# One part of k squared moved ahead of a z, the last row's order rewritten, and attention weights times v computed as 64x64 blocks

## What is computed

```
mod = silu(c) @ wmod                     # shifts, scales and gates, one set for each row
h   = layernorm(x) * (1 + ca) + sa
q, k, v = split(h @ w_qkv + b_qkv)       # 8 heads of 64 channels
scores  = einsum("bhld,bhle->bhde", q, k) / 8       # 64 x 64 for each head: channel by channel
attn    = softmax(scores)
a   = einsum("bhld,bhde->bhle", v, attn) @ w_fc + b_fc + h
x   = x + ga * (layernorm(a) * gamma + beta)
h   = layernorm(x) * (1 + cb) + sb
xr, xk = mixes of h with h shifted by one position (mu_r, mu_k)
x   = x + gb * sigmoid(xr @ W_r) * (relu(xk @ W_k)**2 @ W_v)
```

## Time and profile before

| | before |
|---|---|
| median of 3 runs | 682.86 us |
| lowest and highest | 682.77 and 684.41 us |
| the profiled execution, its own time | 681.41 us |
| its span in the profile | 679.5 us |
| TensorE busy | 653.2 us, 96% |
| VectorE busy | 567.5 us, 84% |
| ScalarE busy | 457.0 us, 67% |
| GpSimd busy | 288.0 us, 42% |
| mean granted TensorE clock | 0.994 of full speed |

### The profile page before, as it was taken

One profiled execution on the slowest core, in us unless ns is written; L12 is line 12 of the kernel. 1 busy time (PEld: TensorE's weight loads), 2 busy tenths in 40 slices (PEclk: granted clock), 3 DMA queues, 4 the chain that ended last, 5 costly groups with the idle time before them and its releaser, 6 DMA issues. The chain is left out here.

```text
span 679.5 us, 12488 instructions
## 1 busy us (share of the span) xinstructions
PE 653.2 (96%) x3968; PEld 535.5 (79%) x3968; DVE 567.5 (84%) x1328; ACT 457.0 (67%) x983; POOL 288.0 (42%) x499
## 2 busy tenths in 40 slices
PE   8987899999999999999999999999999999999896
PEld 6776777888869887889868888788878898697665
DVE  5994988889788988899798897889888997858973
ACT  1423686776957688666967779567876769667662
POOL 5272632753228242662318532382327543214320
PEclk9979999999999999999999999999999999999999
DMA  8749336584945867294855759268663727538225
GB/s 317 240 151 207 125 101 124 93 181 110 202 100 91 223 121 183 42 186 135 191 95 101 188 116 205 70 127 205 138 147 66 135 72 171 102 74 186 31 33 92
DMA packets 90985, 93.04 MB, mean 137 GB/s; under 512 B 4224, under 2 KB 89000, under 8 KB 90960
## 3 DMA queue, kind: packets, MB, share of 16 engines
q0 software_dynamic: 33264, 33.03, 33.0%
q1 hardware_dynamic: 55344, 55.97, 25.8%
q10 hardware_dynamic: 2352, 3.73, 1.5%
HBM read 42.84 MB, written 33.10 MB: 112 GB/s over the span
## 5 line engine op out<-in xcount | busy, mean ns | idle before, releaser
L478 POOL TENSOR_TENSOR rs<-ve,neg_half 128x4 f32<-128x4 f32 x32 | 38.9, 1215 | 183.5 <-DVE ve L944 183.5
L1424 PE MATMUL work<-mx,w_k_t 128*128 128x512 f32 x244 | 109.9, 592 | 0.0
L1407 PE MATMUL work<-w_r_t,mx 128*128 128x256 f32 x464 | 105.9, 381 | 0.0
L717 ACT ACTIVATE z<-x,nm,rs 128x256 f32<-128x256 f32 x128 | 66.3, 593 | 48.6 <-POOL nm L480 48.6
L1407 PEld LDWEIGHTS work<-w_r_t,mx 128*128 128x128 f32 x464 | 85.8, 190 | 11.2 <-DVE y L1008 0.3
L1354 PE MATMUL gram<-z 128*128 128x256 f32 (+1 forms) x512 | 89.1, 327 | 0.0
L1354 PEld LDWEIGHTS gram<-z 128*128 128x128 f32 x512 | 79.8, 191 | 6.6
L1424 PEld LDWEIGHTS work<-mx,w_k_t 128*128 128x128 f32 x244 | 46.3, 190 | 46.0 <-issue 42.0
L1238 PE MATMUL att<-m_lo,z_hi 128*128 128x256 f32 x248 | 74.2, 299 | 4.2 <-DVE t_buf L923 2.2
L1238 PE MATMUL work<-wvf_lo,k_hi 128*128 128x256 f32 x248 | 72.3, 291 | 5.9 <-DVE k_lo L999 3.1
L1239 PE MATMUL att<-m_hi,z_hi 128*128 128x256 f32 x248 | 70.0, 282 | 0.0
(11 more groups left out here) (186 smaller groups left out, 1595.4 us busy)
## 6 DMA issues: line engine op xcount, KB each, us to landing
x_in<-in_L_attn_x_dram SPq DMA_DIRECT2D x32, 512.0 KB, 5.0
x<-rows SPq DMA_DIRECT2D x32, 512.0 KB, 3.5
x<-in_L_attn_x_dram POOLq DMA_DIRECT2D x32, 512.0 KB, 8.8
out_dram<-x SPq DMA_DIRECT2D x31, 512.0 KB, 5.1
out_dram<-y POOLq DMA_DIRECT2D x29, 512.0 KB, 5.9
rows<-row_scratch SPq DMA_DIRECT2D x16, 128.0 KB, 5.2
rows<-row_scratch SPq DMA_DIRECT2D x8, 256.0 KB, 4.0
wqkv_sb<-in_L_attn_w_qkv_dram ACTq DMA_DIRECT2D x1, 1536.0 KB, 9.7
```

What stands on the lines that cost most here:

```text
L717: ins = nc.scalar.activation(z2[:, t], x2[:, j, t], ACT.Identity, bias=nm_2[:, s, t:t + 1], scale=rs_2[:, s, t:t + 1])
L1407: ins = mm(r_banks(alone)[q][:, (t % 2) * D:(t % 2 + 1) * D], mixed(j)[0][:, ch, tile], w_r_t[:, ch], start=(ch == 0), stop=(ch == KD - 1))
L1424: ins = mm(k_banks(alone)[dh][:], w_k_t[:, ch, rows_dh], mixed(j)[1][:, ch], start=(ch == 0), stop=(ch == KD - 1))
```

## The change

It has three parts.

1. In rows 1 to 6, on VectorE, `low_k(b - 1, 3)` stands ahead of `make_z(n, 2)` and no longer behind it.
2. The last row's list is rewritten on four engines. TensorE: `turn_z2(b, 0)` ahead of `ffn_out(b - 1, 3)`, and `ffn_r(b, 0)`, `turn_z2(b, 1)` ahead of `attention(b, 3)`. ScalarE: `make_z2(b, 0)` between the halves of `take_k(b - 1, 3)`, `copy_h2(b, 0)` ahead of `squares(b, 2)`, `take_r(b, 0)` and `copy_h2(b, 1)` ahead of `squares(b, 3)`. VectorE: `mix_alone(b, 0)` and `gate_o(b - 1, 3)` ahead of `make_x2(b, 2)`. GpSimd: `rstd_2(b, 1)` ahead of `rstd_o(b, 2)`, `rstd_2(b, 2)` ahead of `rstd_o(b, 3)`.
3. `wv_attn` computes only the diagonal blocks: eight products of a 64x64 block with 256 columns in place of four of 128x128. The block g = 1 writes to the other bank than g = 0, so the pairs in rows 64 to 127 of `pv_t` lie exchanged, and the load of `w_fc` puts its rows 64 to 127 exchanged as well, in three transfers in place of one. `pv_done` is raised once, by 2, at the last product. Its waits stand in a step of their own, `wait_attn`; in a row this comes first, then `turn_z2(b, 3)`, then the products, then `make_m`.

The diff, cut to its core:

```
@@ gpsimd, last_row
                 add_y(b - 1, 2)
+                rstd_2(b, 1)
                 rstd_o(b, 2)
-                rstd_2(b, 1)
+                add_y(b - 1, 3)
+                rstd_2(b, 2)
                 rstd_o(b, 3)
-                rstd_2(b, 2)
-                add_y(b - 1, 3)
                 rstd_2(b, 3)
@@ scalar, load_more
-                act.dma_start(wfc_c[:], w_fc.rearrange("(n p) d -> p n d", p=P)).then_inc(wfc_loaded, 16)
+                fc_v = w_fc.rearrange("(n g p) d -> g p n d", g=2, p=DX)
+                act.dma_start(wfc_c[0:DX], fc_v[0]).then_inc(wfc_loaded, 16)
+                for q in range(2):
+                    act.dma_start(wfc_c[DX:P, 2 * q:2 * q + 2], fc_v[1, :, 2 - 2 * q:4 - 2 * q]).then_inc(wfc_loaded, 16)
@@ scalar, last_row
                 take_r(b - 1, 3)
-                take_k(b - 1, 3)
+                take_k(b - 1, 3, halves=(0,))
+                make_z2(b, 0)
+                take_k(b - 1, 3, halves=(1,))
+                copy_h2(b, 0)
                 squares(b, 2, alone=True)
-                make_z2(b, 0)
-                copy_h2(b, 0)
                 make_z2(b, 1)
+                take_r(b, 0)
+                copy_h2(b, 1)
                 squares(b, 3, alone=True)
-                copy_h2(b, 1)
-                take_r(b, 0)
                 make_z2(b, 2)
@@ vector, row_steps
+                    low_k(b - 1, 3)
                     make_z(n, 2)
-                    low_k(b - 1, 3)
@@ vector, last_row
                 low_k(b - 1, 3)
-                make_x2(b, 2, alone=True)
-                mix_alone(b, 0, made=3)
+                mix_alone(b, 0, made=2)
                 gate_o(b - 1, 3)
+                make_x2(b, 2, mixes=1, alone=True)
                 stats_2(b, 2)
@@ tensor
-            def wv_attn(b):
-
+            def wait_attn(b):
                 pe.wait_ge(attn_ready, b + 1)
                 pe.wait_ge(wv_ready, b + 1)
+
+            def wv_attn(b):
                 for p in range(NP):
-                    ins = mm(att[p // 2][:, (p % 2) * D:(p % 2 + 1) * D], attn[:, p], wv_aug[:, p], start=True, stop=True)
-                    if p % 2:
-                        ins.then_inc(pv_done, 1)
+                    for g in range(2):
+                        rows_g = slice(g * DX, (g + 1) * DX)
+                        ins = mm(att[p // 2 ^ g][rows_g, (p % 2) * D:(p % 2 + 1) * D], attn[rows_g, p, rows_g], wv_aug[rows_g, p],
+                                 start=True, stop=True)
+                ins.then_inc(pv_done, 2)
@@ tensor, row_steps
                 ffn_k(b, 2)
+                wait_attn(n)
+                turn_z2(b, 3)
                 wv_attn(n)
-                turn_z2(b, 3)
                 make_m(n)
@@ tensor, last_row
                 attention(b, 2, alone=True)
+                turn_z2(b, 0, last=True)
                 ffn_out(b - 1, 3)
-                turn_z2(b, 0, last=True)
+                ffn_r(b, 0)
+                turn_z2(b, 1, last=True)
                 attention(b, 3, alone=True)
-                turn_z2(b, 1, last=True)
-                ffn_r(b, 0)
                 ffn_k(b, 0)
```

More of the change, by code:

```diff
@@ L886, in centre_fc @@
             def centre_fc():
-                dve.wait_ge(wfc_loaded, 16)
+                dve.wait_ge(wfc_loaded, 48)
                 nc.vector.tensor_reduce(fc_mean[:], wfc_c[:], AX, ALU.add).then_inc(fc_step, 1)
@@ L1565, in _ @@
             turn_ffn()
+            wait_attn(0)
             wv_attn(0)
```

## The result

The changed kernel takes 692.09 us (median of 6 runs, 691.15 to 696.32); the kernel before takes 683.37 in the same comparison (6 runs, 681.50 to 684.41). The ratio is 1.0144, with a 95% interval of 1.0122 to 1.0167: slower by 1.4%, some 9.8 us (the two medians lie 8.7 us apart). The prediction was 692.3 us (680.3 to 696.0) with 0.71 for slower. The profiled execution took 691.60 us, of which 689.6 are its span (before 681.41 and 679.5).

What follows compares the result with a forecast made beforehand. TensorE was taken as the bound, busy 653.2 of 679.5 us. Part 3's 12.9 less part 1's 3.1 and part 2's 0.4 gave +9.4 us, 692.3 us on the median, range 680.3 to 696.0.

Steps and rivals of the forecast that it cites:

- the large term: Part 3, the 64x64 blocks in wv_attn: a loss of 1.73 us in seven rows and 0.8 in the prologue, 12.9 us.
- the half steps without a partner: In the block products, half a step at each end of the group runs unpaired, adding 0.2 us to 1.72.
- (a): Faster: block products run four at a time, 0.43 us a group, 680.3 us; chance 0.17 with any other way to faster.
- (b): No change: the blocks take half the time, 0.86 us a group, sum +0.9, 683.8 us; chance 0.12.
- (c): Much slower: the array's halves do not overlap, 3.44 us a group, sum +21.5, 704.4 us; chance 0.06.
- Changing the block size: Between the transposes and the block products, the switch of block size costs TensorE 0.09 us; the change back is hidden.
- The copies: Before make_m, both copies of the products' banks start behind the last product, leaving TensorE idle 1.44 us a row.
- W: Time of the group of sixteen block instructions in wv_attn, two at a time: 1.92 us, bounds 1.72 and 2.07.
- its own sign of error: The prediction is wrong if a new wait appears at attention(b, 2), among other signs.
- (d): The t_buf behind part 1 eats its refund and the last row gains nothing: +12.9, 695.8 us; chance 0.08.
- the term's lower bound: In the last row, a loss of 0.6 us if rstd_o is slowed by 1 us on GpSimd.
- The transfers of w_fc: In the prologue, two more issues of 0.40 us delay ScalarE's first copy, absorbed by VectorE's 1.12 us idle: nothing, else 0.8.

Runs made afterwards that it cites:

- the kernel that has both: The changed kernel with part 3 undone, parts 1 and 2 staying: 679.17 us, ratio 0.9957 to the kernel before.
- the means above: Mean start of make_m(0): 53.41 in seven kernels with the prologue of before, 54.74 in three with blocks and their loads in the changed kernel's form.
- the run with later issues: The changed kernel with the three w_fc transfers issued behind ScalarE's first two z_hi copies, not ahead of them: 691.72 us, ratio 1.0138 to the kernel before.
- seven kernels with one prologue: Before, parts 1 and 2 alone and together, new order with whole products, and two making z of chunk 2 later: make_m(0) starts at 52.39 to 54.56.

## Why the prediction was right, and where its terms were off

The sum was +9.4 us, and the ratio gives +9.8. The mechanism of the large term was right: products that gain nothing, and copies that nothing covers. That the two times (692.1 against 692.3) lie only 0.2 us apart is luck: part 3 came out some 0.5 us below its forecast, parts 1 and 2 above theirs (by 1.3 us measured one by one, by 0.6 in the kernel that has both), and the kernel before measured 683.37 and not the 682.86 on which the prediction was put.

**The pace of the blocks** was forecast at 1.92 us and is 1.78. The parts of the group in the changed kernel, its first two, its first four and its last two:

```profile
604.59 0.43 PE L1485 MATMUL att<-wv_aug,attn 64*64 64x256 f32 x2
...
604.59 0.65 PE L1485 MATMUL att<-wv_aug,attn 64*64 64x256 f32 x4
...
606.15 0.38 PE L1485 MATMUL att<-wv_aug,attn 64*64 64x256 f32 x2
```

The two of a pair start together (0.007 us apart in the trace). There are eight pairs, seven steps over 1.56 us: the first is 0.27 (0.65 - 0.38), the six behind it 0.216 each, the step of the whole products. With a last step of 0.216 that is 1.78. So the step of 0.215 was right, two at a time was right, and the half steps without a partner that I added, 0.2 us, do not exist. What the group takes longer than the 1.72 of before is 0.05 us at its first step, behind the change of block size. The scores show it too (in the trace of before their first step is 0.107 us, the later ones 0.058); the prediction had read it there as up to 8% in the pace. Rivals (a), (b) and (c), four at a time, half the time and no overlap, fall with these rows. The Trainium skill (TensorEngine Tiling (Array Packing), Theoretical Speedup) gives up to 2x for one dimension of at most 64 and a larger factor where both are small; the quarter of the time that the prediction estimated from it does not hold for these diagonal blocks. They take 1.78 us where the whole products took 1.72, and the measurement decides.

**Changing the block size.** From the transposes' start to the blocks' start 604.59 - 603.62 = 0.97: the 0.88 and 0.09 of the prediction. The 0.05 us at the blocks' first step come on top, and are counted above.

**The copies** were forecast at 1.44 us from the end of the last block's step to `make_m`: the step ends at 604.59 + 1.78 = 606.37, `make_m` starts at 607.72, so 1.35. Of it 0.21 to the first copy (forecast 0.20), 1.08 the copies (1.10) and 0.06 to `make_m` (0.14). The row's sum is 0.97 + 1.78 + 1.35 = 4.10 and not 4.33, and the loss 1.50 and not 1.73. It is the same from `ffn_k` to `make_m`: 597.66 - 591.62 = 6.04 before, 607.72 - 600.19 = 7.53 after. In seven rows the sum was 1.6 us too large: 1.0 from the half steps in W, 0.6 from the copies.

**Part 1** was forecast at 3.1 us with 0.1 of each row's 0.5 perhaps handed on. Beside part 3 it returns 80.09 - 79.67 = 0.42 us a row, 2.5 in six rows, and alone it measured 2.9. I was wrong about its two halves: the wait was worth some 0.7 a row, and 0.33 went on to `attention(b, 2)`, the new wait that the prediction named as its own sign of error. Rival (d), all of it eaten, falls.

**Part 2** was forecast at a gain of 0.4 and gave none. The step that failed is that the `t_buf` of chunk 3 would come at 638.0 in place of 638.9. `turn_z2(b, 2)` came at 637.20, within the 637.1 to 637.5 written down; but `rstd_o`, 0.70 + 1.39 us on GpSimd behind `rstd_2`, let `t_buf` start only at 637.30 of the old clock (before 637.22) and end at 638.96, and `ffn_r(b, 1)` behind it started where it always had. Of this, `rs_o`'s 1.39 us in place of 1.01 is 0.4; so even without it the `t_buf` would have ended near 638.6, and the sum was too short by itself. The slower `rs_o` is the mechanism that I had as the term's lower bound.

**The transfers of w_fc** were forecast at nothing, 0.8 if their cover were gone. The step that failed is their size: two more issues at 0.40 each. They took 0.70 and twice 0.65, since the first is not the old one either, and the first copy came 1.8 us late, not 0.8. VectorE's 1.12 us of idle time did take up its part: its `z_lo` is 2.07 us late (24.64 against 22.57), the `z` behind it 0.89 (25.84 against 24.95). But ScalarE is late as well, and VectorE then waits for it at a place where before it did not wait:

```profile
27.97 1.28 DVE L1050 SCALAR_TENSOR_TENSOR wqk_aug<-wqkv_sb,d_now,wqk_aug 128x1024 f32<-128x1024 f32 x1 [0.75 <-ACT res L713]
```

Before, this starts at 26.25, so the delay is 1.72 us again; the prediction had followed it through VectorE alone. The prologue's loss is 1.3 us by the means above, against the 0.8 of the prediction; in the two traces it looks like 2.6, because the clock added the rest.

In sum: part 3 was forecast at +12.9 and measured +12.4, part 1 at -3.1 and measured -2.9, part 2 at -0.4 and measured +0.75, which its interval does not tell from nothing.

What stays open is how much of a run's time the transfers cost in the end. In the traces they hold back the prologue's scores and products with v by 1.1 to 1.3 us, and later issues return that; but the time of the run with later issues (1.0138 against 1.0144) cannot tell a microsecond, and in its trace, as in that of the changed kernel, the clock is at the lower level for most of the products with v.

## What to carry to other kernels

Before a product is cut into blocks of the array, ask what it shortens: here the zeros beside a diagonal block cost no time of their own, and two diagonal blocks side by side took what the whole product took, and copies that must now wait for the last block need work beside them. Work that can stand between a group of products and their use is worth most just there; ahead of the group it covered nothing here. And a step moved out of one wait's way may have been filling another: look at what its engine would wait for at the old place before it is moved.

## What the runs showed of the hardware that I had not expected

- Two products of 64 rows and 64 columns in opposite corners of the array start together, and such pairs follow in steps of 0.216 us for 256 columns of fp32, the step of a whole 128x128 product; the first step behind a change of block size is 0.27. With all of one corner first, each corner keeps the step of 0.216 to itself, and the second corner's list begins beside the fifth of the first corner's eight instructions, so that the sixteen start over 2.48 us and not 1.56.
- The issue of a transfer to 64 partitions on ScalarE's queue held it 0.64 to 0.70 us; that of the same matrix to 128 partitions in one piece held it 0.40.
- The same instructions at the same place of the prologue took 2.12 us in one execution and 3.56 in another, at granted clocks of 1.00 and 0.50 over 50 to 53 us, and `make_m(0)` of seven kernels with one prologue spread over 2.2 us. A difference between two traces' prologues that is smaller than this says nothing about an edit by itself.
